# Diagonal matrices made by ScalarE, a query filter made by VectorE, and small weights reordered in three expert layers

## What is computed

```python
# L0 ffn: 16 experts, each takes its 64 best tokens
prob = softmax(x @ Wg + bg); w = prob kept where a token is among the expert's 64 best, else 0
out = sum_e w[:, e] * (relu(relu(x @ w1[e] + b1[e]) @ w2[e] + b2[e]) @ w3[e] + b3[e])

# L1 attention: gated delta rule with convolutions
q, k, v = (silu(conv4(x @ W, taps)) for the three of them)      # causal filters of 4 taps
delta = delta_rule(l2norm(q), l2norm(k), v * beta, k * beta)     # chunks, triangular inverse
ms = (conv3(v), conv15(v), conv31(v)) @ mix @ mixer              # causal filters per channel
wts = softmax(gelu([x, mean|ms|, mean|delta|, mean|v|] @ fw1 + fb1) @ fw2 + fb2)
out = rmsnorm(wts0 * ms + wts1 * delta + wts2 * v) @ Wo

# L1 ffn: 8 experts, two per token
h[e] = gelu(layernorm(x @ w1[e] + b1[e]) * g1[e] + b1n[e])
out = layernorm(x + sum_e w[:, e] * (h[e] @ w2[e] + b2[e])) * out_g + out_b

# L3 ffn: 8 experts, one per token
xe = layernorm(x) * g[e] + b[e]; y[e] = x + relu(xe @ w1[e] + b1[e]) @ w2[e] + b2[e]
```

## Time and profile before

| what | us |
|---|---|
| median of 3 runs | 2479.2 (2478.42 to 2498.26) |
| the profiled execution, its own time | 2480.31 |
| its span, from the first instruction to the last | 2478.5 |
| TensorE busy | 2297.5 (93%) |
| VectorE busy | 1686.0 (68%) |
| ScalarE busy | 1490.3 (60%) |
| GpSimd busy | 432.2 (17%) |
| mean granted TensorE clock | 0.956 of 2.4 GHz |

### The profile page before, as it was taken

The page is one execution under the profiler, slowest core; times in us unless marked ns, Lnnn a source line. Parts: engine busy times, 40 slices in busy tenths (PEclk is TensorE's granted clock), DMA queues, the critical chain, the costliest instruction groups (busy, mean ns, idle before and its releaser), DMA issues. The chain is left out here.

```text
span 2478.5 us, 68793 instructions
## 1 busy us (share of the span) xinstructions
PE 2297.5 (93%) x26865; PEld 1882.0 (76%) x26865; DVE 1686.0 (68%) x4005; ACT 1490.3 (60%) x2989; POOL 432.2 (17%) x365
## 2 busy tenths in 40 slices
PE   6999999888999999999678899999977999999968
PEld 5888888786777777777555688888865888888758
DVE  5777777637888888888643677777745777777632
ACT  2666666635777777777213466666642666666611
POOL 3221212002112121210301212122102211222000
PEclk8999999999999999999878899999987999999969
DMA  6577676374434434341132767776615777766335
GB/s 135 108 123 124 123 124 110 48 220 142 128 95 116 108 104 121 91 118 39 45 110 74 132 121 121 121 120 113 98 50 110 134 123 119 115 122 121 54 109 190
DMA packets 151311, 277.55 MB, mean 112 GB/s; under 512 B 32702, under 2 KB 71951, under 8 KB 151067
## 3 DMA queue, kind: packets, MB, share of 16 engines
...
...
## 5 line engine op out<-in xcount | busy, mean ns | idle before, releaser
L1151 DVE TENSOR_REDUCE L0x_tops<-L0x_m_bank 128x1 f32<-128x448 f32 x448 | 262.4, 618 | 128.7 <-PE L0x_m_bank L915 126.4
L1151 DVE TENSOR_REDUCE L2x_tops<-L2x_m_bank 128x1 f32<-128x448 f32 x448 | 262.5, 618 | 127.1 <-PE L2x_m_bank L915 125.0
L1151 DVE TENSOR_REDUCE L3x_tops<-L3x_m_bank 128x1 f32<-128x448 f32 x448 | 262.5, 618 | 126.3 <-PE L3x_m_bank L915 124.0
L456 ACT ACTIVATE L1x_prob<-L1x_p_s,L1x_neg_max 128x512 f32<-128x512 f32 (+1 forms) x400 | 274.9, 687 | 120.2 <-DVE L1x_neg_max L567 117.4
L562 DVE CUSTOM_DVE_ANT_0 L1x_p_s<-L1x_p_s,L1x_mask 128x512 f32<-128x512 f32 (+1 forms) x400 | 273.4, 684 | 36.2 <-PE L1x_p_s L321 31.0
L1050 ACT ACTIVATE L3x_prob<-L3x_s_bank 128x512 f32<-128x512 f32 x448 | 219.4, 542 | 91.3 <-PE L3x_s_bank L926 90.2
L1050 ACT ACTIVATE L0x_prob<-L0x_s_bank 128x512 f32<-128x512 f32 x448 | 219.4, 542 | 90.4 <-PE L0x_s_bank L926 89.0
L1050 ACT ACTIVATE L2x_prob<-L2x_s_bank 128x512 f32<-128x512 f32 x448 | 219.4, 542 | 87.9 <-PE L2x_s_bank L926 86.6
L330 PE MATMUL L1x_p_t<-net_ident,L1x_prob 128*128 128x128 f32 x1568 | 239.0, 273 | 11.0 <-ACT L1x_probT L175 10.9
L330 PEld LDWEIGHTS L1x_p_t<-net_ident,L1x_prob 128*128 128x128 f32 x1568 | 192.0, 140 | 49.3 <-ACT L1x_probT L175 14.4
L321 PE MATMUL L1x_p_s<-L1x_k_stack,L1x_q_stack 96*128 96x512 f32 (+1 forms) x400 | 182.2, 456 | 1.9 <-DVE L1x_q_stack L546 1.9
...
## 6 DMA issues: line engine op xcount, KB each, us to landing
...
```

The lines of the kernel that those rows point to most:

```text
L456: e.activation(prob[:, h % P_RING, 0:nk], p_s[h % S_RING][:, 0:nk], ACT.Exp, bias=neg_max[:, odd, h:h + 1]).then_inc(sem("exped"), 1)
L1151: e.tensor_reduce(tops[:, b % 2, h, half:half + 1], m_bank[n % RING][:, 0:HALF], AX, ALU.max).then_inc(sem("m_free"), 1)
```

## The change

- L1a, GpSimd to ScalarE: each diagonal matrix is one ScalarE copy of the identity with a tap as its scale, in six groups of 8, 8, 12, 12, 12 and 10. Two groups stand ahead of the levels, one behind the copy of Y in each of levels 1 to 4. TensorE waits for a whole group at its first matrix.
- L1a, GpSimd to VectorE: Q's filter is `short_taps(Q, 0, 4)` in level 1. All steps of Q move one level later, the short filters' taps are spread anew over the levels, and the masks of the local scores move behind the last level.
- L1a, TensorE: keep-busy matmuls go from 4, 6, 20, 8 to 4, 0, 8, 10 ahead of the levels; 5 and 18 are added in the tail. The Gelu table is loaded by a dummy activation.
- L1f: `b1` is fetched as eight transfers that repeat a row of 2 KB over 128 partitions, on ScalarE's queue; VectorE adds it while it takes `h` from PSUM. The bias matmuls and ScalarE's copies go. The gate's choice moves behind the addition of expert 3.
- L0f, L1f, L3f: SP issues only the gate's matrix ahead of the large weights. The rest goes to ScalarE's queue with semaphores of its own.

```diff
@@ token_choice_experts (L0f)
-            for t, src in ((wg, chunked(w["wg"])), (bg, w["bg"]), (b12, w["b12"]), (b3, w["b3"])):
-                e.dma_start(t[:], src).then_inc(sem("gate_weights"), 16)
+            e.dma_start(wg[:], chunked(w["wg"])).then_inc(sem("gate_loaded"), 16)
...
             norm_scalar(e, m, "ln", scratch)
+            for t, src in ((bg, w["bg"]), (b12, w["b12"]), (b3, w["b3"])):
+                e.dma_start(t[:], src).then_inc(sem("gate_weights"), 16)
@@ top_two_experts (L1f)
-                e.matmul(p_h[x_ % 2][:], ones[:], b1[:, x_, :], start=True, stop=False)
                 for c in range(DC):
-                    i = e.matmul(p_h[x_ % 2][:], xnT[:, c, :], w1[:, x_, c, :], start=False, stop=c == DC - 1)
+                    i = e.matmul(p_h[x_ % 2][:], xnT[:, c, :], w1[:, x_, c, :], start=c == 0, stop=c == DC - 1)
...
             norm_scalar(e, m, "ln", scratch)
+            for x_ in range(E):
+                e.dma_start(b1[:, x_, :], w["b1"][:, x_, :].broadcast_to([P, H])).then_inc(sem(f"b1_loaded_{x_}"), 16)
...
-            for x_ in range(E):
-                e.wait_ge(sem("h_made"), x_ + 1)
-                e.copy(h[:, x_], p_h[x_ % 2][:]).then_inc(sem("h_copied"), 1)
+            for t, src in ((g1, w["g1"]), (b1n, w["b1n"]), (b2, w["b2"]), (out_g, w["out_g"]), (out_b, w["out_b"])):
+                e.dma_start(t[:], src).then_inc(sem("small_weights"), 16)
...
             for x_ in range(E):
+                e.wait_ge(sem(f"b1_loaded_{x_}"), 16)
+                e.wait_ge(sem("h_made"), x_ + 1)
+                e.tensor_tensor(h[:, x_], p_h[x_ % 2][:], b1[:, x_, :], ALU.add).then_inc(sem("h_copied"), 1)
+                if x_ == 3:
+                    e.wait_ge(sem("exped"), 1)
...
@@ delta_rule_attention (L1a)
-DIAG_AT = (0, 16, 31, 47, 62)
+DIAG_AT = (0, 8, 16, 28, 40, 52, 62)
...
-            keep_busy(e, bank[7], ident, 6)
             e.wait_ge(sem("xnT_copied"), 1)
...
-            keep_busy(e, bank[7], ident, 20)
+            keep_busy(e, bank[7], ident, 8)
...
-            keep_busy(e, bank[7], ident, 8)
+            keep_busy(e, bank[7], ident, 10)
...
+            keep_busy(e, bank[5], ident, 5)
             e.wait_ge(sem("means_made"), 1)
...
+            keep_busy(e, bank[6], ident, 18)
             e.wait_ge(sem("o_done"), 1)
...
+            def spread_taps(g):
+                for k in range(DIAG_AT[g], DIAG_AT[g + 1]):
+                    c, j = divmod(k, TAPS[2])
+                    e.activation(diag[:, c, j, :], ident[:], ACT.Copy, scale=taps[2][:, c, j:j + 1]).then_inc(sem("diag_made"), 1)
...
             e.activation(act[:, K], conv[:, K], ACT.Sigmoid).then_inc(sem("k_sigmoid"), 1)
+            spread_taps(0)
...
             e.activation(root[:, K], ss[:, K], ACT.Sqrt).then_inc(sem("k_roots"), 1)
+            spread_taps(1)
...
+                if level <= 4:
+                    spread_taps(level + 1)
...
+            e.activation(table[:], beta[:, 0:1], ACT.Gelu)
             e.wait_ge(sem("weights"), ALL)
             e.wait_ge(sem("hid_made"), 1)
...
                 if level == 1:
-                    convolve(0, 1)
+                    e.wait_ge(sem("pre_copied"), 3)
+                    short_taps(Q, 0, 4)
+                    e.nop().then_inc(sem("q_convolved"), 1)
@@ nearest_expert (L3f)
-            for t, src in small:
-                e.dma_start(t[:], src).then_inc(sem("small_weights"), 16)
+            e.dma_start(cent[:], chunked(w["cent"])).then_inc(sem("cent_loaded"), 16)
...
             norm_scalar(e, m, "ln", scratch)
+            e.dma_start(g[:], w["g"]).then_inc(sem("affine_loaded"), 16)
+            e.dma_start(b[:], w["b"]).then_inc(sem("affine_loaded"), 16)
             norm_scalar(e, m, "ln2", scratch2)
+            e.dma_start(b1[:], w["b1"]).then_inc(sem("bias_loaded"), 16)
+            e.dma_start(b2[:], w["b2"]).then_inc(sem("bias_loaded"), 16)
```

144 lines of the change are left out of this document (60 added, 84 removed).

## The result

The changed kernel takes 2451.7 us (median of four runs, 2445.06 to 2457.77) against 2481.1 for the kernel before (2478.42 to 2498.26). The ratio is 0.9877, with a 95% interval of 0.9831 to 0.9924. The forecast was 2450, and 2443 to 2462. The profiled execution has a span of 2448.8 us, 29.7 less than before, and a mean clock of 0.962 (0.956).

What follows compares the result with a forecast made beforehand. The prediction took GpSimd's stall of VectorE in L1a's front as the largest hole, then TensorE as bound. Terms L1a -14.6, L1f -11.5, L3f -3.1, L0f -0.2 sum to -29.4 us from 2480.3, forecasting 2450 us, range 2443 to 2462.

Steps and rivals of the forecast that it cites:

- What bounds the kernel, and the front of L1a: L1a start: GpSimd's multiplications stall VectorE's V filter and idle TensorE; removing them ends the front 12.0 us earlier (10.4 to 13.4).
- Diagonals: L1a levels: ScalarE makes diagonals at 0.29 us each, delaying copies of Y in levels 2 and 3; +1.0 us (0 to +2.6).
- Rival 2: L1a levels: ScalarE becomes the bound at 0.40 us per diagonal, some 4 us more, total 2454; chance 0.12.
- Tail: L1a end: Gelu table loaded ahead and keep-busy matmuls hold the clock up; -3.2 us (-1.3 to -3.5).
- The share of the five ahead of the twelve-row product: L1a tail: five keep-busy matmuls keep the clock up, so the twelve-row product gains 0.7 us.
- everything at full clock: L1f's first loop: starts at 1285.0, eight experts take 15.3 us plus a 0.5 wait, ends at 1300.8; -13.9 us.
- the old clock: L1f's first loop: clock rises only at 1297 as before, loop ends at 1306.7; -8.0 us, with -7 as weak bound.
- rival 1: L1f: bias transfers hold back w1 to every 2.7 us, loop ends 2.5 us later than at best; chance 0.15.
- The term of a group: L1f's first loop: the four records of one expert's weights take 1.91 us at full clock.
- 1.91 us of need per expert is not far below: L1f: argument against bias transfers delaying w1, setting 1.91 us needed per expert against the DMA share already above 1.0.
- The term of the weights: L3f: four small transfers leave SP's queue, so TensorE's wait for the second expert's weights falls by 1.8 us.
- the gate chain is late next: L0f: TensorE waits for the gate's `taken`, not the weights, limiting the gain to -0.2 us (-0.7 to +0.7).

Runs made afterwards that it cites:

- the kernel before with the late GpSimd: The kernel before, with one wait so GpSimd makes its last three diagonal groups only after VectorE finishes V's filter; L1a took 87.7 us.

## Why the prediction was right, and where only its number was

*What bounds the kernel, and the front of L1a.* Right, and shown by the runs with GpSimd: the stall was GpSimd's. Six taps take 1.91 us, as forecast, V was turned inside the forecast bounds (15.2 to 16.5 us, measured 15.7), and the front ends 11.7 us earlier (forecast 12.0). The prediction named the ten keep-busy matmuls "at a clock that may be low"; it was low, and against the run that filled the gap that costs 1.3 to 2.7 us. Two sizes inside the front were off and made up for each other: the projections start 2.4 us earlier (1.7 in the sum), but their 24 records take 5.70 us at the low clock instead of 3.41.

*Diagonals.* 0.30 us each where 0.29 was taken. Levels 2 and 3 came 0.6 and 0.4 late (0.7 and 0.5). But from the first copy of Y to the mixing it is 30.97 us against 30.80, so +0.2 where the sum had +1.0 - 0.4 = +0.6: levels 4 and 5 were shorter (4.69 and 4.91 against 5.13 and 5.08), Q's turns and the filter's matmuls had been dealt out anew over the levels, which the sum did not look at. Rival 2 (0.40 each) is out.

*Tail.* From the mixing to the end -3.6 us, forecast -3.2. The table is worth its 1.28 us: the Gelu starts 0.1 us after the product's last record, and of the two kernels without keep-busy matmuls in the tail, the one that loads the table ahead is 1.28 us shorter there. The Trainium skill's drain of 1.38 us ("ScalarE: Activation LUTs", section "What ACT_TABLE_LOAD costs") is not in these rows. Beyond the table, 1.7 us are the clock's, as the run without the keep-busy matmuls shows, and 0.6 are the slow twelve-row product of the profile before, which the change didn't cure. The share of the five ahead of the twelve-row product, 0.7 in the sum, was mis-assigned: the product was fast without them too, and fast in the kernel before with the late GpSimd (1.15 us). Its slowness in the stretch of the earlier trace rows belonged to that one execution. Against a kernel before without it, the tail's gain is 3.0 us.

*L1f: right number, wrong reason.* The forecast of -11.5 was a value between "everything at full clock" (-13.9) and "the old clock" (-7 to -8). The measured -11.2 is neither. The clock was 1.00 throughout the loop, and the loop still ended 23.7 us into the module, where the sum at full clock had 21.8 (6.0 + 15.8). The reason is rival 1: w1 every 2.6 to 2.8 us from expert 1 to expert 4, as that rival had worked out (2.7, with the end at 24.4). It had a chance of 0.15, and its mechanism is what happened, at the full clock and not with the old one. The early start of this profile (4.5 us in, not 6.0, since the twelve keep-busy records ahead took 1.50 us and not 2.33) paid nothing back: in seven of the eight profiles of this code the loop starts at 4.5 to 6.5 us, and in all seven it ends at 23.7 to 23.9. Its end is set by the transfers. The term of a group was mis-sized too, on the safe side: 1.72 us, not 1.91, which had been read behind a one-row pair. The step that failed is the sentence "1.91 us of need per expert is not far below": at 0.75 MB per expert and 391 GB/s [the row of 1272 to 1280] the need is 2.0 us of transfer alone, and it starts late. Bytes over rate, from rows 10, would have said this ahead. How near the number came is in part luck: against the other profile of the old L1f (65.5 us) the median gain is 8.8, not 11.4.

*L3f.* -3.2 for -3.1 is luck. The first group began 0.9 us earlier in the module and the second 1.5, not 1.8. The other 1.6 was the clock that held. In the twelve profiles with this code the module took 75.0 us in the median, and only two were under 73.5. The term of the weights is 1.5 us; the clock's 1.6 can't be counted on.

*L0f.* -0.6 in the profile, -0.5 in the median, inside the bounds (-0.7 to +0.7). `taken` is used 13.5 us in (14.0). The forecast was that the gate chain is late next. In this profile it is not: `taken` was there at 13.1, and TensorE's last wait ahead of it is 1.43 us for a `w`. In five other profiles of this code TensorE does wait for `taken`, 0.25 to 1.20 us. So both are near, and the small gain fits either.

*The whole.* With medians in place of single profiles the four terms are -0.5, -15.6, -11.4 and -1.5, -29.0 together. The kernel before stands in them with one profile; with L1f at 65.5 the sum is -26.4. Against 29.4 and 23.8 us in the two comparisons, both sums fit within the intervals. That the first comparison gave just the 29.4 of the forecast's sum is luck.
